# Mixture of experts and gated recurrence in one kernel: another order of sections, earlier shared units, and recurrence steps issued in halves

## The reference

```python
shared = silu(xf @ w1) * (xf @ w3) @ w2
s = sigmoid(concat([xf, tf], -1) @ router_W)              # 8 experts
topk_idx = top_k(s + router_bias, 2)                      # two experts per token
gates = s_sel / (s_sel.sum(1) + 1e-9)
h = gelu(einsum('nc,ech->enh', xf, W1e)); y = einsum('enh,ehc->enc', h, W2e)
x = x + (shared + einsum('ne,enc->nc', combine, y)) / 3
# second layer, over time, h starts as cond:
gate = sigmoid(h @ Wh.T + z_t @ Wz.T + b)
h = tanh(h * (1 - alpha) + gate * z_t)                    # z_t is layer 1's output at step t
x = x + h_t
```

## Time and profile before

| | us |
|---|---|
| time before, median of 3 runs | 876.31 (873.49 to 877.86) |
| profiled execution, span from first to last instruction | 964.0 |
| TensorE busy | 771.4 (80%) |
| VectorE busy | 531.1 (55%) |
| ScalarE busy | 461.6 (48%) |
| GpSimd busy | 272.8 (28%) |
| mean granted TensorE clock | 0.897 |

### The profile page before, as it was taken

How to read it: one execution, slowest core, us unless ns; L and a number is a source line. 1 busy time by engine, 2 the same in 40 slices (tenths; PEclk the granted TensorE clock), 3 DMA queues, 4 the chain that set the end, 5 groups by cost and what they waited for, 6 DMA issues and landing times.

```text
span 964.0 us, 23915 instructions
## 1 busy us (share of the span) xinstructions
PE 771.4 (80%) x8642; PEld 547.5 (57%) x8642; DVE 531.1 (55%) x1974; ACT 461.6 (48%) x1332; POOL 272.8 (28%) x286
## 2 busy tenths in 40 slices
PE   2368857777999969998886999888698999998553
PEld 1135646643587735587763558675355887465332
DVE  4546413444766436758444777644477545677444
ACT  3345523243555534565552566555255666455233
POOL 2244403655203453401325330233432000432000
PEclk9679978798989998999998999989799999999555
DMA  7985999548637432955532484753253452222001
GB/s 194 364 257 121 210 206 216 168 148 178 156 85 188 137 116 72 208 110 140 161 116 88 97 189 78 157 125 127 77 121 88 90 139 98 90 72 66 1 12 45
DMA packets 180195, 127.99 MB, mean 133 GB/s; under 512 B 132434, under 2 KB 160884, under 8 KB 180084
## 3 DMA queue, kind: packets, MB, share of 16 engines
q1 hardware_dynamic: 164420, 83.39, 36.7%
q0 software_dynamic: 14400, 41.96, 13.8%
q10 hardware_dynamic: 1264, 1.10, 0.5%
HBM read 39.90 MB, written 55.84 MB: 99 GB/s over the span
## 4 chain that ended last, share of the span: by engine, by line
PE 52%; DVE 17%; ACT 10%; another core or an unknown queue 7%; issue 6%; SPq 4%; DMA 3%; DVEq 0%; ACTq 0%
PE bank L1550 51%; SPq L814 3%; DVE hid_low L1335 2%; DVE pre L1384 2%; DVE taken L1381 2%; ACT th L1093 2%; DMA y_got<-in_L_cond_W1e_dram 2%; DVE o_ch L1404 2%; ACT hs_high L1101 2%; DVE r_sum L1354 1%; PE bank L1722 1%; DVE r_part L1350 1%; ACT hid_high L1046 1%; DVE hs_low L1390 1%
## 5 line engine op out<-in xcount | busy, mean ns | idle before, releaser
L1550 PE MATMUL bank<-xe,w1e_high 128*128 128x128 f16 x1360 | 223.2, 227 | 22.4 <-DMA xe<-x_slots_even 7.1
L1550 PE MATMUL bank<-xs,w_high 128*128 128x512 f16 x512 | 176.3, 392 | 21.9 <-ACT full L1062 12.8
L1093 ACT ACTIVATE th<-bank 128x64 f32<-128x64 f32 x256 | 57.3, 224 | 226.7 <-PE bank L1550 171.0
L1335 DVE TENSOR_TENSOR hid_low<-full,hid_high 128x512 f16<-128x512 f32 (+1 forms) x152 | 103.0, 677 | 105.8 <-ACT hid_high L1046 75.3
L1550 PE MATMUL bank<-xe,w1e_low 128*128 128x128 f16 x680 | 150.7, 226 | 1.7 <-issue 1.6
L1381 DVE SCALAR_TENSOR_TENSOR taken<-th,zq 128x64 f32<-128x64 f32 x256 | 57.3, 224 | 171.2 <-ACT th L1093 151.6
L1550 PEld LDWEIGHTS bank<-xe,w1e_high 128*128 x1360 | 120.9, 101 | 42.0 <-issue 27.7
L1550 PE MATMUL bank<-hs_high,gwt_high 128*128 128x32 f16 x1024 | 80.4, 180 | 76.8 <-ACT hs_high L1101 63.3
L1550 PEld LDWEIGHTS bank<-hs_high,gwt_high 128*128 128x128 f16 x1024 | 69.6, 99 | 114.3 <-ACT hs_high L1101 84.0
L1101 ACT ACTIVATE hs_high<-pre 128x64 f16<-128x64 f32 x256 | 65.6, 256 | 99.3 <-DVE pre L1384 90.8
L1550 PE MATMUL bank<-xs,w_low 128*128 128x512 f16 x256 | 100.4, 392 | 0.3 <-issue 0.3
(11 more groups left out here) (152 smaller groups left out, 1746.1 us busy)
## 6 DMA issues: line engine op xcount, KB each, us to landing
y_slots_even<-y_pair SPq DMA_DIRECT2D x41, 256.0 KB
y_slots_odd<-y_pair SPq DMA_DIRECT2D x41, 256.0 KB
x_tok<-in_x_dram SPq DMA_DIRECT2D x16, 512.0 KB
x_res<-in_x_dram SPq DMA_DIRECT2D x16, 512.0 KB
out_dram<-o_tok SPq DMA_DIRECT2D x32, 256.0 KB
x_slots_even<-zeros POOLq DMA_DIRECT2D x1, 3072.0 KB, 16.1
x_slots_odd<-zeros POOLq DMA_DIRECT2D x1, 3072.0 KB, 23.5
y_got<-in_L_cond_W1e_dram SPq DMA_DIRECT2D x4, 512.0 KB, 20.3
```

The source lines that it names most:

```text
L1093: nc.scalar.activation(flat3(th[:, s % 2]), gate_sums(s), ACT.Tanh, scale=0.5 / UP).then_inc(s_th, 1)
L1335: dve.tensor_tensor(hid[1][:, u.i % NR, some], full32[:, u.i % 2, some], hid[0][:, u.i % NR, some], ALU.subtract).then_inc(s_lo, 1)
L1550: return pe.matmul(out_ap, w, mov, start=start, stop=stop, skip_group_check=True)
```

## The change

The sections become 8, 12, 12, 12, 12, 8 tiles. The order of units is now written out (`ORDER`): shared 0-7 (section 0), shared 8-11 (the first group of section 1), pairs 12-23 (section 0), shared 24-31 (the rest of section 1), pairs 32-63 (sections 1 and 2), shared 64-75, pairs 76-91, shared 92-103, pairs 104-119, shared 120-131, pairs 132-143, shared 144-151. The numbers of SHARED and EXPERT units stay 64 and 88.

Groups whose shared units come before the section's pairs (`AHEAD`, groups 0 to 4) get their routed rows later through `spare` (`SUM`, `sum_routed`, `add_part`). The logits of section 0 move from ahead of the units to unit 1, its routing into units 2 to 6 (`first_section`). Two loads of x move from SP to ACT; the loads and splits of weights are spread over units 0 to 10; the second clearing of `x_slots` comes after the first scatters. `gate_step` is cut in two, `HIGH` (8 matmuls) and `STEP` (4), each with its own wait; a fill is cut in two halves; TensorE gets a gap after every pass of three, so up to some 30 gaps per unit. The tables are written anew. New waits: SP's first store of a section's pairs waits for the section before last's gathers to be summed (`s_r`), POOL's first scatter of a section for the pairs two sections back (`s_up`). `zq` has 6 buffers for 5, `zs` 3 for 4.

```diff
-SECTIONS = (8,8,12,12,12,12)
+SECTIONS = (8, 12, 12, 12, 12, 8)
+ORDER = ((SHARED, 0, 0, 8), (SHARED, 1, 0, 4), (EXPERT, 0, 0, 12), (SHARED, 1, 4, 12), (EXPERT, 1, 0, 16),
+         (EXPERT, 2, 0, 16), (SHARED, 2, 0, 12), (EXPERT, 3, 0, 16), (SHARED, 3, 0, 12),
+         (EXPERT, 4, 0, 16), (SHARED, 4, 0, 12), (EXPERT, 5, 0, 12), (SHARED, 5, 0, 8))
+for _q, _u in {0: 27, 1: 31, 2: 55, 3: 59, 4: 63}.items():
+    FINISH[_q] = _u
+SUM_AT = {_q: [FINISH[_q] + 2, FINISH[_q] + 3] for _q in range(N_GROUPS) if AHEAD[_q]}
+PREP_UNIT = dict(zip(range(N_GROUPS), (-1, -1, -1, -1, 3, 18, 22, 27, 44, 46, 48, 70, 72, 76, 100, 102)))
-LOGITS_UNIT = [-3, 2] + [START[_n - 1] + 1 for _n in range(2, NS)]
+LOGITS_UNIT = [1, 10, 31, 51, 78, 105]
+SCATTER_AT = [[_f + _j * _a // _b for _j in range(_n)] for _n, _f, _a, _b in zip(
+    SECTIONS, (6, 16, 36, 58, 85, 112), (1, 1, 8, 3, 15, 15), (2, 2, 12, 4, 12, 8))]
 PE_AT = {
-    (34, 5): ((FILL, 0), (STEP, 0),), (34, 8): ((FILL, 1),), (35, 2): ((STEP, 1),), (35, 4): ((STEP, 2),),
+    (31, 3): ((FILL, 0), (FILL, 1), (FILL, 2), (FILL, 3), (HIGH, 0), (STEP, 0),), (31, 9): ((HIGH, 1),),
...
-    (149, 5): ((STEP, 212),), (150, 1): ((STEP, 213),), (150, 4): ((STEP, 214),), (151, 3): ((STEP, 215),),
+    (46, 4): ((HIGH, 31),), (46, 5): ((STEP, 31),),
+    (60, 1): ((FILL, 8), (FILL, 9), (FILL, 10), (FILL, 11), (HIGH, 32), (STEP, 32),), (60, 7): ((HIGH, 33),),
...
+    (120, 29): ((HIGH, 175),), (120, 30): ((STEP, 175),),
+    (126, 14): ((FILL, 44), (FILL, 45), (FILL, 46), (FILL, 47), (HIGH, 176), (STEP, 176),), (127, 1): ((HIGH, 177),),
...
+    (146, 14): ((HIGH, 223),), (146, 15): ((STEP, 223),),
+    (150, 14): ((FILL, 56), (FILL, 57), (FILL, 58), (FILL, 59), (HIGH, 224), (STEP, 224),), (151, 1): ((HIGH, 225),),
...
-        NZQ = 5
+        NZQ = 6
-        NZS = 4
+        NZS = 3
-        CONV_SLOT = [-1] * NSTAGE + [0, 1, 2, 3, 4, 5, 6]
+        CONV_SLOT = [-1, -1, 0, 1, 2, 4, 6, 7, 8, 9, 10]
             def store_pair(u):
+                if u.k == 0 and u.n >= 2:
+                    sp.wait_ge(s_r, TILE0[u.n - 1])
...
-            for q in range(TILE0[1] // GROUP):
-                turn_x(q)
-            load_weight(N_ACT_LOADS)
+            turn_x(0)
+            for n in range(N_ACT_LOADS, NSTAGE):
+                load_weight(n)
+            turn_x(1)
...
-            clear_slots(1, 1, 0, PAIRS[1])
...
+                    if n >= 2:
+                        pool.wait_ge(s_up, FIRST_PAIR[n - 2] + PAIRS[n - 2])
                     pass_fence()
...
+            for q in range(NXT):
+                act.wait_ge(s_xlo, 2 * q + 2)
+                act.dma_start(x_tok[:, q].rearrange("p j c -> p (j c)"), x_in[q + NXT]).then_inc(s_x[q], 16)
             for n in range(N_ACT_LOADS):
                 conv(n)
+            for q in range(NXT, N_FIRST):
+                for i in range(2):
+                    x_high(q, i)
             act.wait_ge(s_condt, 1)
-            act_sigmoid(0)
-            for n in range(N_ACT_LOADS, NSTAGE):
-                conv(n)
...
+                            if n < 2 and (to_up or to_down):
+                                gap()
...
-            def gate_step(s):
-                for c, weights, ready in ((0, (0, 1), s_hhi), (1, (0,), s_hlo)):
-                    pe.wait_ge(ready, s + 1)
+            def gate_part(s, c, weights, ready):
+                pe.wait_ge(ready, s + 1)
...
+            def gate_high(s):
+                gate_part(s, 0, (0, 1), s_hhi)
+            def gate_step(s):
+                gate_part(s, 1, (0,), s_hlo).then_inc(s_step, 1)
+            def sum_routed(q, kc):
+                for j in range(GROUP):
+                    if kc == 0:
+                        pe.wait_ge(s_r, q * GROUP + j + 1)
+                    last = mm(spare[:, j * P:(j + 1) * P], r_sum[:, j, kc * P:(kc + 1) * P], ident_keep[:], True, True)
+                last.then_inc(s_half if kc == 0 else s_y, 1)
-            misc(LOGITS, 0)
             for u in UNITS:
                 body(u)
```

More of the change, by code:

```diff
@@ L671, in released @@
                 eng.wait_ge(s_lg, part + 1)
+            elif what == SUM:
+                eng.wait_ge(s_z, part[0] * KC + part[1] + 1)
             else:
@@ L807, in turn_x @@
             def turn_x(q):
-                if q >= NXS:
-                    sp.wait_ge(s_up, FIRST_SHARED[q - NXS] + MID)
+                before = [r for r in range(q) if PLACE[r] == PLACE[q]]
+                if before:
+                    sp.wait_ge(s_up, FIRST_SHARED[before[-1]] + MID)
+                elif PLACE[q] == NXS - 1:
+                    scattered(sp, section_of(EXTRA * GROUP))
+                    turned(sp, EXTRA)
                 for i in range(2):
@@ L879, in body @@
                     store(MISC[u.i][1])
-                for n in range(2, NS):
-                    if u.i + NEXT_LEAD == FIRST_PAIR[n]:
+                for n in range(NS):
+                    if u.i + NEXT_LEAD == FIRST_PAIR[n] and not follows(n):
                         first_pairs(n)
@@ L1138, in body @@
                 if u.kind == SHARED:
+                    if u.run == 0 and u.i > 0:
+                        for pair in (u.i - DOWN_LAG, u.i - 1):
+                            result(units_at(pair, EXPERT))
+                            gap()
                     silu(u)
@@ L1147, in body @@
                 done = units_at(u.i - DOWN_LAG, EXPERT)
-                if done and (u.kind == EXPERT or u.k == 0):
+                if done and u.kind == EXPERT:
                     result(done)
-                    if u.kind == SHARED:
-                        gap()
-                        result(units_at(u.i - 1, EXPERT))
                 gap()
-                for n in range(1, NS):
+                for n in range(NS):
                     if u.i == LOGITS_UNIT[n] + 1:
@@ L1408, in out_channels, with first_section @@
                 ins.then_inc(s_och, 1)
+            def first_section(u, where, gap):
+                at = 3 * (u.i - LOGITS_UNIT[0]) + where
+                ranked = 3 * RANKS_AFTER[0] + 2
+                for part in range(4):
+                    if at == part + 5:
+                        if part == 0:
+                            dve.wait_ge(s_rbias, 16)
+                            dve.wait_ge(s_ident, 8)
+                        route(0, 3 * part, 3 * part + 2, gap)
+                    if at == ranked + part:
+                        place(0, 3 * part, 3 * part + 2, gap)
             def prepare(at, i):
@@ L1717, in misc @@
                     last.then_inc(s_rkps, 1)
+                elif what == SUM:
+                    sum_routed(*part)
                 else:
```

963 lines of the change are left out of this document (502 added, 461 removed), and 6 rows, old and new, of the table OUT_AT.

## The result

The changed kernel has a median of 878.86 us (870.48 to 884.82), the kernel before, timed beside it, 873.94 us. The ratio is 1.0041 (95% interval 1.0024 to 1.0058): 0.4% slower, by my own bound of 0.5% no change. Forecast were 812 us. The profiled execution took 884.82 us itself, the slowest of its 20 and 6 us above the median; its span is 883.1 us.

The account below looks back on a forecast made before the run. TensorE was taken to set the pace from 261 to 876 us, behind a data-bound head. Terms 29 + 22 + 8 + 14 - 2 = 71 us took 964.0 to 893 us, times 0.909 is 812 us; range 782 to 855.

Parts of the forecast that it names:

- What bounds the kernel now: Whole kernel: waits for data up to 207.3 us, TensorE sets the pace from 261 to 876 us, then the recurrence's tail.
- the ratio 0.909: Timed median over profile span, 876.31 / 964.0; it scaled the forecast span of 893 us to 812 us.
- The start: Up to the first pair: first silu at 21 us, first pair at 77 for 106.2 us; gain 29 us, bounds 5 and 36.
- Rival (a): Head held by DMAs: start gains only 5 us and pairs 10, giving 844 us; chance 0.17.
- The pairs: Pairs of sections 0 and 1: late slot rows and some unnamed stalls go; gain 22 us, bounds 5 and 42.
- The dense part: 261 to 876 us: fewer TensorE waits for hs_low and hs_high; gain 8 us, bounds 35 of gain and 96 of loss.
- units and steps are level at about 2.06 us: Units 60 to 120: TensorE's work and 144 steps take equally long per step, so any chain delay delays TensorE.
- Rival (e): Nothing comes of it: what is saved ahead of the recurrence is given back waiting for z of sections 1 and 3; chance 0.03.
- TensorE's waits: Dense part: of 24.7 us for hs_high and 5.8 for hs_low, the 5.8 go and half of the other 16.
- The tail: After unit 151 begins: 31 steps left instead of 41, about 75 us to the end; gain 14 us, bounds 5 and 20.
- The extra work: Five groups through `spare` and new waits on `s_r` and `s_up`: cost 2 us, or 10 if the cover goes.

Follow-up runs that it names:

- second profile: The kernel before, with no edit, profiled once more: span 871.5 us, where its first profile had 964.0; timed 875.17 us, ratio 0.9997.
- half of the data: Changed kernel, each load of a pair after the first four turning one tile, not two: 871.31 us; with eleven pairs' stores halved too: 873.51 us.
- relieved TensorE: Pairs of sections 3 and 4 with one pass less and no register instructions: 878.09 us in the changed kernel, 870.48 us in the kernel before.

## Why the prediction was wrong, point by point

**The base.** "What bounds the kernel now" read the first profile, and the term for the pairs (22 us) and the ratio 0.909 went by it. The pairs' term counted stalls that timed runs don't have. I had seen that the span was 87.7 us over the median, and scaled the gain by 0.909 in place of striking the stalls out of it. This is the first step that failed, but not the larger one: from the median, without the 22 us, the same sum gives 876.3 - 49 = 827 us, still 52 us below the 878.9 measured.

**The start** (29 us). The first silu came sooner, and the changed kernel's ScalarE shows it:

```profile
26.11 1.28 ACT L1136 ACT_TABLE_LOAD   x1 [4.98 <-PE bank L1638]
27.41 0.60 ACT L1136 ACTIVATE full<-bank 128x512 f32<-128x512 f32 x1
```

27.4 us, for 37.8 before in the second profile (38.46 in the earlier trace rows); I had said 21. But the first pair is not set by how early shared units run. It waits for routing, scatters and loads, and these the change had moved back: GpSimd scatters section 0's rows from 60.6 to 81.1 us, where the kernel before (second profile) does from 41.8 to 73.5. The first pair is at 100.3 us, where I had said 77 and called everything over 95 wrong, and against the second profile the start gains nothing (100.2 for the same work). The four more shared units only fill that time. Rival (a), the head held by DMAs, named the right place: share 0.88 up to 100.3 us and 1.04 in units 48 to 59; but half of the data gained only a few us there.

**The pairs** (22 us). Besides the stalls, two signs failed: section 0's twelve pairs take 54.1 us (100.3 to 154.4), 4.5 apiece and not 3.2, and where section 2 follows section 1 TensorE waits four times for `xe`, 11.3 us in all, where I had said never.

**The dense part** (8 us). Here lies the step that decided: "units and steps are level at about 2.06 us". I had priced the recurrence's stops, units 47 to 59, 121 to 125 and 147 to 149, at nothing, since I took TensorE's work for the bound. The runs show the recurrence as the bound between the stops, and then each stop, a wait of the recurrence for the units, is on the path: 71.0 + 28.0 + 21.0 = 120 us, where the kernel before passes the same three steps in 3.0, 2.8 and 3.8 us. Against that stand a start 9.3 us earlier, 32.2 us on the first 31 steps and 57 us on the 221 steps behind step 32: in sum some 12 us longer, since the same three steps cost the other 9.6 us. The pace was inside what I had named as signs, at its edge, but not the 2.06 us of the sum: 142 tanhs in units 60 to 119, 326.5 / 142 = 2.30 us each (I had said 2.0 to 2.3, wrong from 2.5), for 308.8 / 116 = 2.66 before. At 2.06 these units would have been 34 us shorter. Rival (e) had named this mechanism and its places (what is saved ahead is given back in the stops); I gave it 0.03, wrote that units would have to lose 40 us for it, and had the end hang on the units, not on the recurrence. What my own numbers allowed was a sum over the recurrence: first tanh, plus 256 times the pace, plus the stops.

**TensorE's waits** were a poor guide to that. In units 60 to 150 of the changed kernel it waited for steps only this long:

```profile
PE bank L1638 <- ACT hs_high L1175: 13.9, 22, 1.8
...
PE bank L1638 <- DVE hs_low L1469: 2.5, 5, 1.0
```

for 24.7 and 5.8 us in the earlier trace rows. Against the second profile of the kernel before (7.7 and 3.5 us in units 60 to 150) `hs_low` gives 1 us back and `hs_high` takes 6 more. These few us show nothing of the recurrence's pace, since TensorE reads as busy while it works at that pace. Leaving out a third of the matmuls of 32 pairs took it from 150.2 to 144.5 us only, and taking 22 us of TensorE's work away left the span as it was.

**The tail** (14 us). 67.9 for 87.8 us, where I had said about 75, with 29 tanhs in it for the 31 forecast: near as a length, wrong as a gain. With the recurrence as the bound, steps moved from the tail into units save nothing by themselves: from step 224 to the last it takes 65.5 us, for 60.0 before.

**The extra work** (2 us) and the halves: no effect that can be told, as said.

**Open.** What makes a dense step 2.25 us long, where two steps of the tail without a fill were 1.82 us apart: the units' work on ScalarE and VectorE, which no run relieved, or the places in the tables. What the stops would give back if the steps were spread over them: the 120 us are counted, no run took them away, and fewer stops could mean a slower pace between them. What holds units 48 to 59 besides the amount of data; why the kernel before gave 6.1 us for the relieved TensorE and the changed one only 1.6; and how much of the 57 us from the first pair behind section 1's (273.4) to step 32 (330.3) the gathers, one per unit, could give back. That last was not tried.

## What to carry to other kernels

When one chain of dependent steps runs through the whole kernel, count the time along it: its start, its pace, each stop for data. An engine that reads 90% busy beside it need not be the bound; relieve it in an experiment, with a control that proves the relief, before building on it. And where a profile's span lies 10% above the timed runs, take a second profile or strike out what has no releaser, but don't scale the forecast by the ratio.

## What the runs showed of the hardware

- One execution can take 964.0 us by its profile, another of the same kernel 871.5. The stalls that I have rows for fell where GpSimd issued gathers and scatters back to back; what causes them was not found.
- TensorE's register instructions can set the pace of a pair: a bare pair with 36 matmuls and 20 register instructions took 3.1 to 3.2 us, with 24 and 20 still 3.0 to 3.2, with 24 and none 1.8 to 2.0. (36 and none was not tried.)
- Four MB of zeros issued 1.5 us ahead of five transposing loads: TensorE waited 13.7 us for the first of them. With the zeros held back until the first four had landed, it waited 4.1 us.
